# Cross attention of the first sequence: three stacked-query homes, its own places in the calendar, keys and values through DRAM in halves and tiles

## The reference, cut to what matters

```python
# x: (8, 512, 512), ctx: (8, 77, 512), 16 heads of 32
x = x + xattn(layernorm(x), ctx, ctx, lens)      # cross attention over 77 context tokens
x = x + ffn(layernorm(x))                        # self attention over 512 tokens

def xattn(Q, K, V, lens):
    q, k, v = heads(Q @ Wq), heads(K @ Wk), heads(V @ Wv)
    A = softmax(where(key_pos < lens, q @ k.T / sqrt(32), -1e20))
    return merge(A @ v) @ Wo

def ffn(h):
    gates, idx = top2(relu(h.mean(1) @ gw1.T + gb1) @ gw2.T + gb2)   # two of 8 experts per sequence
    q, k, v = (h @ W_eff(p, idx, gates).T + b for p in "qkv")        # Wm + gated U S V of rank 16
    out = softmax(q @ k.T) @ v
    return out @ W_eff("o", idx, gates).T + ob
```

## Time and profile before

| what | value |
|---|---|
| median of 3 runs | 1584.63 us (1583.43 to 1590.57) |
| profiled execution, its own time | 1589.63 us |
| its span, first to last instruction | 1587.8 us |
| TensorE busy | 1436.1 us, 90% |
| VectorE, ScalarE, GpSimd busy | 1091.5, 818.1 and 619.5 us |
| mean granted TensorE clock | 0.933 of full |
| chain that ended last, TensorE's share | 72% |

### The profile page before, as it was taken

How to read it: one execution, slowest core, us unless ns; L and a number is a source line. 1 busy time by engine, 2 the same in 40 slices (tenths; PEclk the granted TensorE clock), 3 DMA queues, 4 the chain that set the end, 5 groups by cost and what they waited for, 6 DMA issues and landing times.

```text
span 1587.8 us, 17048 instructions
## 1 busy us (share of the span) xinstructions
PE 1436.1 (90%) x5624; PEld 707.8 (45%) x5624; DVE 1091.5 (69%) x1780; ACT 818.1 (52%) x1426; POOL 619.5 (39%) x381
## 2 busy tenths in 40 slices
PE   5667799989998999989998999899998999799877
PEld 3332444444544454444544454445544454345322
DVE  2223556787778877887778777887778777786542
ACT  0221445565556655556547555666456554645531
POOL 3001102452445444542345245544445244554553
PEclk9865899999999999999999999999999999899867
DMA  5512222251232431342235223243134222512110
GB/s 189 124 28 84 85 52 54 71 159 42 74 104 76 112 81 50 101 121 71 57 90 150 52 75 102 63 109 84 51 101 134 63 58 56 136 39 76 45 50 27
DMA packets 73311, 130.81 MB, mean 82 GB/s; under 512 B 22710, under 2 KB 25398, under 8 KB 70151
## 3 DMA queue, kind: packets, MB, share of 16 engines
q1 hardware_dynamic: 69127, 128.66, 30.5%
q10 hardware_dynamic: 4096, 1.06, 0.3%
HBM read 66.08 MB, written 12.21 MB: 49 GB/s over the span
## 4 chain that ended last, share of the span: by engine, by line
PE 72%; DVE 12%; DMA 5%; SPq 4%; ACT 4%; issue 2%; POOL 0%; ACTq 0%; DVEq 0%; POOLq 0%
PE pj L1009 36%; PE sc L1063 7%; PE scT L1091 7%; PE acc L1120 6%; PE sc L1052 4%; DVE uv_stack L938 4%; DVE negmax L840 2%; PE pj L1038 2%; PE pj L1129 2%; PE scT L1084 2%; PE pj L1100 2%; PE pj L1003 2%; PE pj L1108 2%; SPq L466 1%; SPq L517 1%
## 5 line engine op out<-in xcount | busy, mean ns | idle before, releaser
L736 ACT ACTIVATE probs<-scT 128x512 f32<-128x512 f32 x512 | 290.7, 594 | 382.9 <-PE scT L1091 377.2
L840 DVE TENSOR_REDUCE negmax<-sc 128x1 f32<-128x512 f32 x512 | 343.2, 684 | 141.4 <-PE sc L1063 139.8
L616 POOL TENSOR_TENSOR probs_sum<-probs_sum,probs 128x1024 f32<-128x1024 f32 x128 | 301.3, 2372 | 59.5 <-ACT probs L736 59.3
L612 POOL TENSOR_TENSOR probs_sum<-probs 128x1024 f32<-128x1024 f32 x64 | 155.2, 2431 | 373.4 <-ACT probs L736 373.4
L1063 PE MATMUL sc<-ks,qs 96*128 96x512 f32 x512 | 283.6, 572 | 13.4 <-DVE negmax L840 6.5
L1091 PE MATMUL scT<-qs,ks 99*128 99x512 f32 x512 | 280.0, 579 | 13.4 <-DMA qs<-shift 10.1
L1009 PE MATMUL pj<-XT,Wqk 128*128 128x512 f32 x512 | 264.0, 602 | 0.1
L867 DVE RECIPROCAL inv_sum<-pj 128x128 f32<-128x128 f32 x256 | 224.1, 919 | 56.2 <-PE pj L1129 37.1
L1063 PEld LDWEIGHTS sc<-ks,qs 96*128 96x128 f32 x512 | 99.8, 198 | 133.5 <-issue 92.0
L1091 PEld LDWEIGHTS scT<-qs,ks 99*128 99x128 f32 x512 | 99.0, 197 | 128.0 <-issue 66.6
L1120 PE MATMUL acc<-probs,V 128*32 128x512 f32 x1024 | 140.1, 632 | 0.0
(11 more groups left out here) (95 smaller groups left out, 1782.5 us busy)
## 6 DMA issues: line engine op xcount, KB each, us to landing
Wqk<-in_WmT SPq DMA_DIRECT2D x16, 1024.0 KB, 6.1
Wvo<-in_WmT SPq DMA_DIRECT2D x16, 1024.0 KB, 5.7
UVS_sb<-in_UVS SPq DMA_DIRECT2D x64, 192.8 KB, 3.4
X<-in_x SPq DMA_DIRECT2D x8, 1024.0 KB, 6.3
qsc<-stage_lo SPq DMA_DIRECT2D x128, 64.0 KB, 2.0
qsc<-qsc SPq DMA_DIRECT2D x32, 256.0 KB, 3.1
qs<-stage_lo SPq DMA_DIRECT2D x128, 64.0 KB, 2.0
qs<-qs SPq DMA_DIRECT2D x32, 256.0 KB, 3.1
```

The costliest lines, as they stand in the source:

```text
L612: nc.gpsimd.tensor_tensor(probs_sum[:, pair], probs[:, 0, pair], probs[:, 1, pair], ALU.add)\
L616: nc.gpsimd.tensor_tensor(probs_sum[:, pair], probs_sum[:, pair], probs[:, kt % 2, pair], ALU.add)\
L736: nc.scalar.activation(probs[:, kt % 2, jj, :], scT[:, ST[step], :], ACT.Exp, scale=SCALE)\
L840: nc.vector.tensor_reduce(negmax[:, 0, n:n + 1], sc[:, SC[step], :], AX.X, ALU.max, negate=True)\
```

## The change

1. `q1_rows` and `q1_stack` of sequence 0 use three homes in turn, `qsc`, `qs[:, 0]` and `qs[:, 1]` (the self attention's query stacks, still unused then). A job waits for the `csT` of the job three before it. All other sequences use `qsc` alone.
2. `split_keys` goes in two halves of four sequences each; a half and part is one DMA, four in all in place of 32, into `k1_hbm` laid out as the SBUF tile is (2, 128, 4, 8, 78). The three key loads of `context` then gather pieces of 78 numbers (312 bytes) where they read rows of 4992 bytes. Each half has its semaphore. The load of values is a step of its own, `context_v`, and waits only for the value tiles it reads; each tile has its semaphore.
3. Initial loads: small constants ahead of the context and Wk1; Wq1 and Wv1 follow with semaphores of their own. TensorE no longer waits for the constant memsets at its start; those of `ks` go from GpSimd to VectorE.
4. `csc` on VectorE also waits until the maxima of the job before are transposed.
5. CALENDAR is new for all sequences, and OWN now places almost every cross step of sequence 0, its gate, and its first weights. Of the value tiles one is made before the queries, one between the score jobs, and three behind `out1` of sequence 0. `residual_bias` moves from just behind the gate (175) to 2996.

```diff
-    "residual_bias": (175,),
+    "residual_bias": (2996,),
 OWN = {
-    "split_keys": {(): -2174},
-    "context_values": {(0,): -2047, (1,): -1980, (2,): -1969, (3,): -1961, (4,): -1827},
+    "split_keys": {(0,): -1991, (1,): -1630},
+    "context_values": {(0,): -2413, (1,): -818, (2,): 73, (3,): 203, (4,): 283},
...
+def home_of(b, i):
+
+    return i % 3 if b == 0 else 0
...
+        def cross_stack(b, i):
+            return (qsc[:], qs[:, 0], qs[:, 1])[home_of(b, i)]
...
-            def split_keys(step):
+            def split_keys(step, half):
                 for part, split in ((0, "k1_hi"), (1, "k1_lo")):
                     sp.wait_ge(split, sp.after(split, *step))
                     src = (K1_hi, K1_lo)[part]
-                    for h in range(H):
-                        at = h % HJ * DH
-                        queue.dma_start(k1_hbm[part, :, :, h, :], src[at:at + DH, h // HJ].bitcast(F32))\
-                             .then_inc(sems["k1_stored"], 16)
+                    queue.dma_start(k1_hbm[part, :, :, 4 * half:4 * half + 4, :],
+                                    src[:, :, 4 * half:4 * half + 4, :].bitcast(F32))\
+                         .then_inc(sems[f"k1_stored{half}"], 16)
...
-                    queue.dma_start(keys1[part * DH:(part + 1) * DH].rearrange("p c j k -> p (c j) k").bitcast(F32),
-                                    k1_hbm[part % 2, :, b]).then_inc(sems["keys1_loaded"], 16)
+                    queue.dma_start(keys1[part * DH:(part + 1) * DH].bitcast(F32),
+                                    k1_hbm[part % 2, :, :, b, :].rearrange("(j d) c k -> d c j k", d=DH))\
+                         .then_inc(sems["keys1_loaded"], 16)
...
             def q1_rows(step, b, i):
-                before = (b, i - 1) if i else (b - 1, DC - 1)
-                act.wait_ge("consts_made", 9)
-                act.wait_ge("scoresT_full", act.after("scoresT_full", "csT", *before, HJ - 1))
+                before = home_before(b, i)
+                act.wait_ge("consts_made", 7)
+                if before:
+                    act.wait_ge("scoresT_full", act.after("scoresT_full", "csT", *before, HJ - 1))
```

More of the change, by code:

```diff
@@ L99 @@
-    "out2": (3308, 3325, 3345, 3345, 3431, 3460, 3470, 3475, 3502, 3545, 3564, 3585, 3627, 3629, 3641, 3679),
-    "residual2": (3360, 3534, 3617, 3683),
+    "context": (-2016,),
+    "context_v": (-1827,),
+    "load": (-1967,),
+    "stats": (-1952, -1933, -1932, -1928),
+    "deviation": (-1903, 74),
+    "normalize": (-1804, 108),
+    "xpose": (-1784, -1760, -1740, -1731, 116, 134, 151, 170),
+    "q1": (-1684, -1681, -1672, -1671, -1669, -1653, -1649, -1637, -1012, -905, -889, -884, -787, -768, -763, -747),
@@ new lines @@
+    "cpv": (-1121, -710, -320, -61),
+    "cacc": (-1121, -683, -238, -43),
+    "cden": (-960, -577, -441, -55),
+    "cinv": (-960, -897, -896, -896, -564, -563, -515, -513, -433, -416, -405, -381, -52, -42, -25, -25),
+    "wm_load": (199, 472, -88, 3053),
+    "cdivide": (-653, -468, -97, -26, -12, -7, 45),
+    "out1": (-38, -19, -3, -3, -140, -96, -45, 18, 26, 52, 52, 52, -3, 39, 58, 58),
+    "residual1": (2, 27, 64, 73),
+    "residual_bias": (2996,),
+    "token_sums": (161, 165, 169, 179),
@@ L130 @@
 QUOTIENTS = [(j, piece) for j in JOBS for piece in range(pieces(j))]
-INDICES = {"context": [()], "load": [()], "stats": product(FOUR), "deviation": product(PAIR),
+INDICES = {"context": [()], "context_v": [()], "load": [()], "stats": product(FOUR), "deviation": product(PAIR),
            "normalize": product(PAIR), "xpose": product(PAIR, FOUR), "q1": product(JOBS, FOUR),
@@ L486, in context, with context_v @@
                      .then_inc(sems["keys1_loaded"], 16)
+            def context_v(step, b):
+                for n, (first, end) in enumerate(CTX_TILES):
+                    if first < (b + 1) * NK and b * NK < end:
+                        sp.wait_ge(f"v1_stored{n}", sp.after(f"v1_stored{n}", "context_values", n))
                 sp.wait_ge("pj_full", sp.after("pj_full", "cpv", b - 1, DC - 1))
@@ L492, in load @@
                     return
-                sp.wait_ge("k1_stored", sp.after("k1_stored", "split_keys"))
+                for half in range(2):
+                    sp.wait_ge(f"k1_stored{half}", sp.after(f"k1_stored{half}", "split_keys", half))
                 sp.wait_ge("mask_stored", 16)
@@ L698, in qk_rows @@
                 before = (b, j - 2) if j >= 2 else (b - 1, j + DC - 2)
-                act.wait_ge("consts_made", 9)
+                act.wait_ge("consts_made", 7)
+                act.wait_ge("ks_made", 2)
+                if b == 0 and w == 0 and j < 2:
+                    act.wait_ge("scoresT_full", act.after("scoresT_full", "csT", 0, j + 1, HJ - 1))
                 act.wait_ge("scoresT_full", act.after("scoresT_full", "sT", *before, TT - 1, HJ - 1))
@@ L829, in csc @@
             def csc(step, b, i, t):
-                dve.wait_ge("consts_made", 9)
+                before = (b, i - 1) if i else (b - 1, DC - 1)
+                dve.wait_ge("consts_made", 7)
+                dve.wait_ge("pj_full", dve.after("pj_full", "cross_shift", *before))
                 dve.wait_ge("scores_full", dve.after("scores_full", *step))
@@ L950, in v_bias @@
             def v_bias(step, b, t):
-                dve.wait_ge("k1_stored", dve.after("k1_stored", "split_keys"))
+                for half in range(2):
+                    dve.wait_ge(f"k1_stored{half}", dve.after(f"k1_stored{half}", "split_keys", half))
                 dve.wait_ge("pv_done", dve.after("pv_done", "pv", b - 1, DC - 2, TT - 1))
@@ L1095, in cpv @@
                 p = opened(("cacc", b, i))
[L1096 removed]
+                pe.wait_ge("v1_loaded", pe.after("v1_loaded", "context_v", b))
                 pe.wait_ge("exp_done", pe.after("exp_done", "csT", b, i, HJ - 1))
```

230 lines of the change are left out of this document (129 added, 101 removed), and 40 rows, old and new, of tables (CALENDAR, OWN).

## The result

The changed kernel takes **1520.42 us** (median of 4 runs, 1518.01 to 1521.45) beside 1584.03 for the kernel before in the same comparison: ratio 0.959, 95% interval 0.957 to 0.962. The forecast was 1532, its range 1504 to 1556. The profiled execution took 1520.18 us with a span of 1518.4; the profiled span of before was 1587.8, so **69.4 us** of the two profiles are to be explained where the sum said 52.7. The profile of before lies 5.0 us above its median; by the medians of this comparison the gain is 63.6 us.

The account below looks back on a forecast made before the run. The middle was taken as bound by TensorE, the first 165 us by something else, with waits for first product, keys and stacks. Minus 23.1, minus 26.6, plus 3, minus 6 gave minus 52.7: median 1532 us, range 1504 to 1556.

Parts of the forecast that it names:

- Part 1: Kernel start: small constants first, Wv1 on its own semaphore; first product at 13.4 instead of 15.96, minus 2.5 us.
- Part 2: Up to the first `csc`: four key stores instead of 32, `csc` at 50.6 instead of 73.7, minus 23.1 us.
- Part 3: First `csc` to `out1`, sequence 0: four jobs with three homes take 49 us instead of 75.6, minus 26.6.
- I take the lower level: Sequence 0's four jobs: TensorE at the lower clock level, 47 us of work plus 2 us for the chain's end.
- Part 4: Behind `out1` of sequence 0: three value tiles, 10.3 us, mostly meet idle time, plus 3 us.
- Part 5: Middle periods and end: new order shortens the wait behind the gate, minus 6 us (minus 15 to plus 1).
- other distances (stacks to scores, ...) keep over what they need by the durations here: Middle periods: other producer-to-consumer distances in TensorE's order differ by one to three us either way but remain sufficient.
- 4.2 becomes 2 to 4.3: Middle periods: TensorE's largest wait, 4.2 us behind the gate, falls to between 2 and 4.3 us, at seven places.
- (a): Rival, chance 0.20: clock stays up in sequence 0's jobs (12 less), gate gives its whole 15 us (9 less): 1511.
- (b): Rival, chance 0.17: homes do not cover, each job still waits, first `csc` at 56, no middle gain: 1552.
- (c): Rival, chance 0.08: small DRAM pieces and SP's order keep the keys out until 60 us: 1541.
- (d): Rival, chance 0.04: SP held at the V weights' load, stacks late for scores, 9 us lost a period: 1601.

## Why the prediction was right, and where it was off

- **Views.** "The middle is bound by TensorE and the first 165 us by something else" held: 56.6 of 69.4 us came ahead of the first gate. "At most 8 us of a period can be won there" did not: with K's weights moved a mean period of the middle takes 164.9 us in place of 173.4, 8.5 less, though TensorE had been idle in only 7.0 of it. Its busy time was partly the clock (0.98), and that could be won too.
- **Part 1,** first product at 13.4: 13.69. No run takes this part back alone.
- **Part 2,** first `csc` at 50.6: 52.20, minus 21.5 in place of minus 23.1. The stack and not TensorE came last, by 1.42 us. With the 32 stores back it came 19.7 later, so SP's 32 issues were the cause.
- **Part 3, the mis-sized term:** minus 26.6 forecast, 42.5 us measured from the first `csc` to the main run of `out1` in place of 75.6, minus 33.1. The step that failed is "I take the lower level" for all of it. The sum had 47 us of TensorE's work at that level and 2 of waiting; there were 38.5 busy and 4.0 idle, with the clock at the upper level up to 55, from 59 to 69 and after 93. I took the level of the old stretch, with 27.0 us of idle time in it, for one that had 4.0. What sets the level inside the jobs stays open. The run with one home has idle time and lower level together (41 us at 0.51). But in the changed kernel the clock fell at 69.0, after 9 us in which TensorE was busy 8.6, and 1.5 us ahead of its next wait, 1.8 us for the stack of job 3; and three tiles more raised it with the idle time unchanged. The bounds (37 to 60) held it. "`out1` keeps its 15.4" failed too: 28 of its 32 matmuls took 12.3 at full clock and four were drawn ahead, another 3.1.
- **Part 4,** plus 3: plus 2.4 (19.8 us behind `out1` in place of 17.4). The walk was right, the cover is real: tiles put elsewhere brought the waits of 4.7 back.
- **Part 5,** minus 6 in sum: minus 14.0 from q1 of sequence 1 on, made of 8.4 up to the second gate, 8.7 behind the last one, and plus 3.1 in the middle. The gate: "if the three last operations of the gate no longer last as long as an addition each" was right in effect (0.16 us each, the wait of 4.2 gone, 5.3 back with the additions), though what lengthens them can be the sums of probabilities as well. The step that failed is "other distances (stacks to scores, ...) keep over what they need by the durations here". I had measured distances on TensorE, and for the stack not what stands ahead of it in SP's queue: 1 MB of weights had moved from well ahead of it to just ahead of it. That wait of 3.6 us, with the clock, cost 9 us a period, and its removal gave 53.9 us in the middle, more than the gate's fix in the same periods (34.7 between the two kernels with K's weights moved). "4.2 becomes 2 to 4.3" was too small a gain: the wait behind the gate, 25.2 us in the six middle periods, is gone.
- **Rivals.** (a) was half true in the jobs; its other half, the whole wait behind the gate, came, and the new wait for the stack, with the clock, took it back. (b) and (c) are out by 52.20 and by the run with 32 stores. (d) looked at SP's order and at the load of the V weights; the real harm was in SP's order too, at the load of K's weights, and smaller than 6.7 us a period net because the gate paid for part of it.
- **The total** lies in the range partly by luck. 1520.42 lies just under the forecast's own range of 1522 to 1543 and a little nearer to (a), 1511, than to 1532. By the profiles the parts up to q1 of sequence 1 gave 8.7 us more than forecast and part 5 another 8.0; the two errors add. What kept the time inside 1504 to 1556 was a loss that no term of the sum had: with K's weights moved, one number, the same kernel takes 1468.61. The new calendar was worth far more than minus 6, and the new wait ate it.

## What to carry to other kernels

Price a TensorE wait of some microseconds in a stretch that is otherwise at full clock at one and a half to two and a half times itself (here, a period: 3.5 us idle and 5.5 lost at half speed behind K's weights, 4.5 and 2.6 in the run with the wait put back), and when a change removes such waits, price the stretch at the clock that it will then have. A second wait in a period that already has one can come cheaper (12.3 us in six periods in place of 34.7). When a large load is moved, look at what is issued within the next few microseconds on the same queue, not only at who needs the load. A new buffer is worth nothing until the order lets it be filled ahead (1.000 with the old order, 34 to 41 us with the new one).

## What the runs showed of the hardware that I had not expected

- Useless matmuls in a gap made the kernel faster: 42.2 us of them in the middle, and the middle 12.4 us shorter, since the same useful work went from 1010.2 to 976.5 us.
- Behind a gap of 3.6 us TensorE worked 1.3 us more at full clock and then 10.2 at 1.2 GHz; in another kernel the clock fell inside the gap of 4.3 us, and 5.2 us of work were at 1.2 GHz. What decides this stays open.
- A VectorE operation on one or two numbers with two inputs took from 0.16 to 2.27 us, depending on whether GpSimd was adding two tensors beside it; one with a single input took 0.17 beside the same addition.
